# Two side products of a head pair change places: batch 1's queries into the third unit, the second half of its keys into the fourth unit's second step

## The chip, the cores and the metric

The kernel runs on one core of one Trainium2 chip. The metric is the device time of one execution in microseconds (us).

## What is computed

A gated layer: `x` (2 batches of 512 tokens, 512 wide, f32) is normed, attends to a context of 1024 tokens of 128 with 16 heads, and is added back under a gate; then a quantised feed-forward layer (512 to 2048 to 512) is added under a second gate. The change touches the attention alone:

```
q_hk = (hidden_q @ Wq.T).reshape(b, s, H, K)
q_big = jnp.einsum('bshk,hkq->bshq', q_hk, w_kc_q)
q_r = jnp.einsum('bshq,hqr->bhsr', q_big, W_qr)
k_r = jnp.einsum('bld,hdr->bhlr', kv_rope, W_kr)
scores = jnp.einsum('bhsr,bhlr->bhsl', q_r, k_r)
attn = jax.nn.softmax(scores, axis=-1)
ctx_c = jnp.einsum('bhsl,bld->bhsd', attn, kv_rope)
ctx_lat = jnp.einsum('bhsd,hkd->bshk', ctx_c, w_kc_kv)
out = ctx_lat.reshape(b, s, H * K) @ Wo.T
```

## The kernel before

The 16 heads are worked on as 8 pairs. Each pair goes through four units, w = 0 to 3: units 0 and 1 are batch 0, units 2 and 3 batch 1, each of 256 query rows for both heads (a buffer E of four 128x1024 tiles). The text calls them first to fourth unit. A unit has eight steps, c = 0 to 7, one per 128 tokens of context, and its steps are numbered from 0 as in the code, except where the change's own words say "second step" (c = 1).

In a step TensorE (`pe_pair`) does, in this order:

- the turn: four 128x128 transposes of E into one PSUM bank (L1350);
- at c = 3 and c = 7 a round of scores (L1297, twelve matmuls) for a unit ahead: at 3 the second half of the next unit, at 7 the first half of the one after it;
- the product of the turned probabilities and the context, two or three steps behind (L1308, L1309, L1310, three matmuls of 512 columns, into `ps_ctx`), none at c = 2, two rounds at c = 5;
- a side task, where the table `SIDE` names one: `("k", b, j)` is half j of the next pair's keys of batch b (L1249 to L1251, three matmuls), `("q", b)` the next pair's queries of batch b (L1270 to L1272, twelve matmuls), `("out", u, s)` the output rows of unit u (L1204 to L1206), `("m",)`, `("a",)` and `("b", h)` products of weights.

Every f32 operand is split into a high and a low part. So the turned bank is read twice: ScalarE copies it to `et_hi` (L1447) and VectorE writes the rest as `et_lo` (L1611), and only then is the bank free. The same goes for a side task of kind a, b, q or k: ScalarE's copy (`side_high`), then VectorE's subtraction (`side_low`, L1611 too). Both engines do this at the start of the step behind the task (`task_before`), ahead of that step's own turn. In between, ScalarE takes the exponential of a score tile at c = 0, 1, 4, 5 (L1490), VectorE a maximum over a score tile twice at c = 0, once at 3 and 4 (L1650), a reciprocal (L1655), and from pair 4 on the rounding of feed-forward weights at c = 5 and 7 (L1672); ScalarE takes those weights' sum or tanh (L1514) at some steps. GpSimd scales E (L1104) and, for pairs 5 and 6, reloads a split copy of x (`load_xn`, L1134).

Turns and side tasks share three PSUM banks in turn, in the order of the list that `bank_users` makes. A user waits until the one three places ahead of it has been read by VectorE:

```
def bank_before(variant, user):
    at = PLACE[variant][user] - BANKS
    ...
    return USERS[variant][at - PLACE0[variant]], False
```

Pairs are of three variants: the first (pair 0), the middle ones (1 to 6; pairs 1 to 3 are a loop of the hardware, 4 to 6 written out), and the last (pair 7), which has no next pair and leaves out m, a, q and k (`side_tasks`).

Of the kernel before, what the change touches and what calls it, by code (L numbers as in the profile page):

```python
# [81 lines left out]
SIDE = [  # L82
# [4 lines left out]
]  # L87
WK_AT = (1, 1)
KV1_AT = (1, 6)
# [1765 lines left out]
```

## Time and profile before

| | |
|---|---|
| runs | 738.93 us, median of 3 (737.99 to 739.98) |
| profiled execution | 739.03 us, its span 736.9 us |
| mean granted TensorE clock | 0.997 of 2.4 GHz |
| busy share of the span | TensorE matmul (PE) 98%, its weight loads (PEld) 72%, VectorE (DVE) 78%, ScalarE (ACT) 66%, GpSimd (POOL) 34% |

The span runs from the first to the last instruction. Busy times are sums over instructions; matmuls overlap in the pipeline (one of 512 columns is shown with 0.39 us while the next starts 0.23 us behind it), so a step's length is read from start to start. The windows view gives, for a stretch of the span, its length first, then each engine's busy time in it.

### The profile page before, as it was taken

What the parts mean: (1) busy time and instruction counts of PE and PEld (TensorE: products, weight loads), DVE (VectorE), ACT (ScalarE), POOL (GpSimd) and SP (SyncE); (2) the same over time, 40 slices, a digit from 0 to 9 for tenths busy, and PEclk for the clock granted to TensorE, in tenths of its full rate; (3) what the DMA queues carried; (4) which work ended last, traced back from release to release, by engine and by line L of the source; (5) the groups of instructions that cost most, each with busy time, mean ns of one, the idle gap of its engine ahead of it and who ended that gap; (6) DMA issues with size and microseconds to landing.
All of it is one profiled execution on the core that took longest, in us unless ns stands there. A gap on an engine that the chain in (4) does not pass through costs nothing.

```text
span 736.9 us, 11967 instructions
## 1 busy us (share of the span) xinstructions
PE 718.6 (98%) x4148; PEld 533.5 (72%) x4148; DVE 573.8 (78%) x1022; ACT 487.7 (66%) x821; POOL 252.8 (34%) x231
## 2 busy tenths in 40 slices
PE   8799999999999999999999999999999999999997
PEld 7577778777877787778778877787777776644553
DVE  5967777776778677776888787878787899999863
ACT  2578765666566656666666666666676756478876
POOL 5744422222222222222122222322322234677651
PEclk9999999999999999999999999999999999999999
DMA  8301073104011401040114212543250001000001
GB/s 303 121 2 58 29 271 143 59 29 157 28 57 28 157 28 57 28 157 31 58 57 146 70 59 103 181 155 120 67 195 4 29 1 57 1 1 29 16 29 44
DMA packets 22124, 58.31 MB, mean 79 GB/s; under 512 B 4033, under 2 KB 7233, under 8 KB 21313
## 3 DMA queue, kind: packets, MB, share of 16 engines
q1 hardware_dynamic: 20176, 45.49, 18.3%
q0 software_dynamic: 784, 10.49, 3.7%
q10 hardware_dynamic: 1120, 1.77, 0.7%
q8 instruction: 26, 0.43, 0.2%
q14 instruction: 18, 0.14, 0.1%
HBM read 51.45 MB, written 6.29 MB: 78 GB/s over the span
## 4 chain that ended last, share of the span: by engine, by line
PE 82%; DVE 9%; ACT 3%; POOL 2%; issue 2%; DMA 2%; POOLq 0%; DVEq 0%; ACTq 0%
PE ps_b L1350 14%; PE ps_s L1297 13%; PE ps_ctx L1308 9%; PE ps_ctx L1310 7%; PE ps_ctx L1309 7%; PE ps_s L568 4%; PE ps_b L1206 4%; PE ps_b L1204 4%; PE ps_b L1205 4%; PE ps_b L1270 2%; PE ps_b L619 2%; PE ps_b L1239 2%; PE ps_b L1272 2%; PE ps_b L1271 2%; PE ps_b L1276 2%
## 5 line engine op out<-in xcount | busy, mean ns | idle before, releaser
L1104 POOL TENSOR_SCALAR E<-E,small 128x1024 f32<-128x1024 f32 x128 | 149.1, 1165 | 418.1 <-DVE small L1655 418.1
L1447 ACT ACTIVATE et_hi<-ps_b 128x512 fp32r<-128x512 f32 x256 | 152.6, 602 | 164.3 <-PE ps_b L1350 164.2
L1611 DVE TENSOR_TENSOR et_lo<-ps_b,et_hi 128x512 fp32r<-128x512 f32 x256 | 175.5, 686 | 53.7 <-ACT et_hi L1447 52.0
L1650 DVE TENSOR_REDUCE small<-ps_s 128x1 f32<-128x1024 f32 x128 | 155.6, 1217 | 4.8 <-PE ps_s L1297 3.4
L1350 PEld LDWEIGHTS ps_b<-ident,E 128*128 128x128 f32 x1024 | 124.8, 140 | 40.0 <-issue 8.8
L1350 PE MATMUL ps_b<-ident,E 128*128 128x128 f32 x1024 | 152.3, 273 | 0.3 <-POOL E L1104 0.3
L1490 ACT ACTIVATE E<-ps_s,small 128x1024 f32<-128x1024 f32 x128 | 142.8, 1116 | 7.7 <-DVE small L1650 7.0
L1308 PE MATMUL ps_ctx<-et_hi,kv_hi 128*128 128x512 f32 x256 | 121.0, 473 | 0.5 <-DVE ctx_lo L1611 0.5
L1310 PE MATMUL ps_ctx<-et_lo,kv_hi 128*128 128x512 f32 x256 | 101.1, 395 | 0.0
L1309 PE MATMUL ps_ctx<-et_hi,kv_lo 128*128 128x512 f32 x256 | 100.5, 393 | 0.0
L1636 DVE SCALAR_TENSOR_TENSOR x_sb<-ps_b,small,x_sb 128x512 f32<-128x512 f32 x62 | 46.3, 746 | 28.5 <-PE ps_b L1206 28.5
L1308 PEld LDWEIGHTS ps_ctx<-et_hi,kv_hi 128*128 128x128 f32 x256 | 48.3, 189 | 24.8 <-issue 15.0
L568 PE MATMUL ps_s<-wq,q12T 128*128 128x512 fp8e4 x256 | 59.9, 379 | 1.3 <-issue 1.2
L1297 PE MATMUL ps_s<-k_hi,q_hi 64*128 64x512 f32 x256 | 57.5, 444 | 3.0 <-ACT E L1490 2.7
L1310 PEld LDWEIGHTS ps_ctx<-et_lo,kv_hi 128*128 128x128 f32 x256 | 48.0, 188 | 11.2
L1297 PE MATMUL ps_s<-k_hi,q_lo 64*128 64x512 f32 x256 | 51.0, 392 | 0.0
L1297 PE MATMUL ps_s<-k_lo,q_hi 64*128 64x512 f32 x256 | 51.0, 392 | 0.0
L1204 PE MATMUL ps_b<-b_hi,ctx_hi 128*128 128x512 f32 x128 | 50.4, 394 | 0.0
L1206 PE MATMUL ps_b<-b_lo,ctx_hi 128*128 128x512 f32 x128 | 50.3, 393 | 0.0
L1309 PEld LDWEIGHTS ps_ctx<-et_hi,kv_lo 128*128 128x128 f32 x256 | 48.8, 191 | 1.5
L1205 PE MATMUL ps_b<-b_hi,ctx_lo 128*128 128x512 f32 x128 | 49.9, 390 | 0.0
L510 POOL TENSOR_TENSOR hg<-h_f,E 128x512 f32<-128x512 f32 x32 | 40.5, 1272 | 22.5 <-DVE h_f L903 22.5
(187 smaller groups left out, 1078.4 us busy)
## 6 DMA issues: line engine op xcount, KB each, us to landing
w_stage<-in_wffn SPq DMA_DIRECT2D x48, 512.0 KB, 3.4
xnT<-xn_split POOLq DMA_DIRECT2D x3, 2048.0 KB, 9.6
wo_s<-in_woT SPq DMA_DIRECT2D x8, 512.0 KB, 7.1
xn_split<-xnT POOLq DMA_DIRECT2D x2, 2048.0 KB, 9.4
wq_s<-in_wq SPq DMA_DIRECT2D x7, 512.0 KB, 6.3
wkcq_s<-in_wkcqT SPq DMA_DIRECT2D x7, 384.0 KB, 4.1
x_sb<-in_x SPq DMA_DIRECT2D x4, 512.0 KB, 5.9
out<-x_sb SPq DMA_DIRECT2D x8, 256.0 KB, 2.0
```

What stands on the lines that cost most here:

```text
L568: last = nc.tensor.matmul(ps_s4[:, 2 * i + c % 2, :], q12T[:, k, i, d, :], wq8[:, DT * i + d, cols], start=(d == 0), stop=(d == DT - 1))
L1104: nc.gpsimd.tensor_scalar(e, e, rowinv[:, k:k + 1], 1.0, ALU.mult, ALU.mult).then_inc(scaled, 1)
L1204: nc.tensor.matmul(into, ctx_hi[:, u % 2, cols], b_hi[:, h, :], start=(h == 0), stop=False)
L1297: last = nc.tensor.matmul(ps_s[:, h, cols], q[head, b, rows], k[head, b, cols], start=(i == 0), stop=(i == 2))
L1308: nc.tensor.matmul(ps_ctx[:, :], kv_hi[:, b, c, :], et_hi[:, c % ET_RING, :], start=(c == 0), stop=False)
L1309: nc.tensor.matmul(ps_ctx[:, :], kv_lo[:, b, c, :], et_hi[:, c % ET_RING, :], start=False, stop=False)
L1310: nc.tensor.matmul(ps_ctx[:, :], kv_hi[:, b, c, :], et_lo[:, c % ET_RING, :], start=False, stop=(c == LT - 1))\
L1350: last = nc.tensor.transpose(into[:, s * P:(s + 1) * P], E[:, w % 2, s, c * P:(c + 1) * P], ident[:, :])
L1447: return nc.scalar.activation(out, in_, ACT.Copy)
L1490: nc.scalar.activation(E[:, w % 2, t, :], ps_s[:, t % 2, :], ACT.Exp, bias=negmax[:, k:k + 1], accum_out=rowsum[:, k:k + 1]).then_inc(exp_ ...
L1611: return nc.vector.tensor_tensor(out, full, hi.bitcast(F32), ALU.subtract)
L1650: nc.vector.tensor_reduce(negmax[:, k:k + 1], ps_s[:, t % 2, :], AX_X, ALU.max, negate=True).then_inc(max_done, 1)
```

## The change

Two entries of the table of side tasks move. `("q", 1)`, batch 1's queries of the next pair, goes from step 1 of the fourth unit to step 6 of the third. `("k", 1, 1)`, the second half of batch 1's keys, goes from step 3 of the fourth unit to step 1, the place that the queries leave.

```diff
 SIDE = [
     {0: ("m",), 2: ("a",), 4: ("out", 3, 0), 5: ("out", 3, 1), 6: ("b", 0)},
     {0: ("b", 1), 2: ("q", 0), 4: ("out", 0, 0), 5: ("out", 0, 1)},
-    {0: ("k", 0, 0), 1: ("k", 0, 1), 4: ("out", 1, 0), 5: ("out", 1, 1)},
-    {0: ("k", 1, 0), 1: ("q", 1), 3: ("k", 1, 1), 4: ("out", 2, 0), 5: ("out", 2, 1)},
+    {0: ("k", 0, 0), 1: ("k", 0, 1), 4: ("out", 1, 0), 5: ("out", 1, 1), 6: ("q", 1)},
+    {0: ("k", 1, 0), 1: ("k", 1, 1), 4: ("out", 2, 0), 5: ("out", 2, 1)},
 ]
```

The list of bank users, the counts that waits compare with and the places of ScalarE's and VectorE's copies all follow from this table. The number of instructions on each engine stays the same.

**TensorE, fourth unit of a pair, from the end of step 1 to the scores of step 3.** Before, the last of the queries' matmuls and the two turns:

```order
L1271 MATMUL ps_b<-xnT1,a_lo 128x512
L1272 MATMUL ps_b<-xnT1,a_hi 128x512
L1350 MATMUL ps_b<-ident,E 128x128 [waits side_freed]
L1350 MATMUL ps_b<-ident,E 128x128 x3
L1350 MATMUL ps_b<-ident,E 128x128 [waits et_split]
L1350 MATMUL ps_b<-ident,E 128x128 x3
L1297 MATMUL ps_s<-k_hi,q_hi 128x512 [waits exp_done]
```

Now:

```order
L1249 MATMUL ps_b<-kvT_hi,wk_hi 128x512 [waits wk_ready,et_split]
L1250 MATMUL ps_b<-kvT_hi,wk_lo 128x512
L1251 MATMUL ps_b<-kvT_lo,wk_hi 128x512
L1350 MATMUL ps_b<-ident,E 128x128 [waits side_freed]
L1350 MATMUL ps_b<-ident,E 128x128 x3
L1350 MATMUL ps_b<-ident,E 128x128 [waits et_split]
L1350 MATMUL ps_b<-ident,E 128x128 x3
L1297 MATMUL ps_s<-k_hi,q_hi 128x512 [waits exp_done]
```

The twelve query matmuls in front of the two turns have given way to three key matmuls. Both turns wait as before: that of step 2 for step 0's keys to be split (`side_freed`), that of step 3 for step 1's own turn (`et_split`).

**VectorE, fourth unit, from step 0's low part to that of step 3.** Before:

```order
L1611 TENSOR_TENSOR et_lo<-ps_b,et_hi 128x512 [waits ethi_done]
L1650 TENSOR_REDUCE small<-ps_s 128x1 [waits scores_done]
L1611 TENSOR_TENSOR k_lo<-ps_b,k_hi 128x512 [waits side_hi]
L1611 TENSOR_TENSOR et_lo<-ps_b,et_hi 128x512 [waits ethi_done]
L1655 RECIPROCAL small<-small 128x1 [waits exp_done]
L1611 TENSOR_TENSOR ctx_lo<-ps_ctx,ctx_hi 128x512 [waits ctxhi_done]
L1611 TENSOR_TENSOR q_lo<-ps_b,q_hi 128x512 [waits side_hi]
```

Now:

```order
L1611 TENSOR_TENSOR et_lo<-ps_b,et_hi 128x512 [waits ethi_done]
L1650 TENSOR_REDUCE small<-ps_s 128x1 [waits scores_done]
L1611 TENSOR_TENSOR k_lo<-ps_b,k_hi 128x512 [waits side_hi]
L1611 TENSOR_TENSOR et_lo<-ps_b,et_hi 128x512 [waits ethi_done]
L1655 RECIPROCAL small<-small 128x1 [waits exp_done]
L1611 TENSOR_TENSOR ctx_lo<-ps_ctx,ctx_hi 128x512 [waits ctxhi_done]
L1611 TENSOR_TENSOR k_lo<-ps_b,k_hi 128x512 [waits side_hi]
```

VectorE's work up to the context's low part is the same; behind it the keys' low part stands where the queries' stood. The row now reads as it does at the same place of the third unit, before and after.

## Rows read from the trace of the kernel before

**Rows 1.** The page: busy time, the span in 40 slices, the chain that ended last.

```profile
PE 718.6 (98%) x4148; PEld 533.5 (72%) x4148; DVE 573.8 (78%) x1022; ACT 487.7 (66%) x821; POOL 252.8 (34%) x231
...
PE   8799999999999999999999999999999999999997
...
PE 82%; DVE 9%; ACT 3%; POOL 2%; issue 2%; DMA 2%; POOLq 0%; DVEq 0%; ACTq 0%
```

**Rows 2.** Windows of pair 4: its third unit, then its fourth (length, busy per engine).

```profile
380.42:397.52 17.10, 17.10 (x100) 13.12 (x99) 14.47 (x25) 12.46 (x21) 4.75 (x4) 1.00 0.19 62
397.52:417.01 19.49, 19.49 (x111) 15.47 (x110) 15.22 (x26) 12.92 (x22) 4.75 (x4) 1.00 0.46 149
```

**Rows 3.** Windows: steps 0 to 3 of that third unit.

```profile
380.42:382.25 1.83, 1.83 (x11) 1.52 (x10) 1.73 (x3) 1.19 (x2) 0.00 (x0) 1.00 0.30 90
382.25:384.17 1.92, 1.92 (x12) 1.39 (x10) 1.92 (x4) 1.92 (x5) 0.00 (x0) 1.00 0.57 188
384.17:384.77 0.60, 0.60 (x6) 0.42 (x5) 0.60 (x2) 0.60 (x2) 0.00 (x0) 1.00 0.00 0
384.77:387.75 2.98, 2.98 (x21) 2.10 (x21) 1.97 (x5) 2.98 (x7) 1.29 (x2) 1.00 0.00 0
```

**Rows 4.** Windows: steps 0 to 3 of the fourth unit of pair 4.

```profile
397.52:399.34 1.82, 1.82 (x12) 1.52 (x11) 1.71 (x3) 1.19 (x2) 0.00 (x0) 1.00 0.47 137
399.34:403.21 3.87, 3.87 (x20) 3.21 (x19) 3.22 (x6) 3.13 (x7) 1.12 (x1) 1.00 0.94 290
403.21:403.64 0.43, 0.43 (x5) 0.43 (x4) 0.00 (x0) 0.23 (x1) 0.00 (x0) 1.00 0.96 334
403.64:407.27 3.63, 3.63 (x25) 2.61 (x23) 2.58 (x5) 2.38 (x4) 1.13 (x1) 1.00 0.68 235
```

**Rows 5.** Windows: a step without a side task (step 6, third unit, pair 4).

```profile
393.46:394.60 1.14, 1.14 (x9) 0.95 (x8) 0.75 (x1) 0.50 (x2) 0.92 (x1) 1.00 0.26 57
```

**Rows 6.** Timeline of steps 0 to 2, third unit, pair 4 (start, duration).

```profile
380.42 0.60 PE L1350 MATMUL ps_b<-ident,E 128*128 128x128 f32 x4
...
381.06 0.60 ACT L1447 ACTIVATE et_hi<-ps_b 128x512 fp32r<-128x512 f32 x1 [1.93 <-PE ps_b L1350]
...
381.69 0.69 DVE L1611 TENSOR_TENSOR et_lo<-ps_b,et_hi 128x512 fp32r<-128x512 f32 x1
...
382.30 1.22 DVE L1650 TENSOR_REDUCE small<-ps_s 128x1 f32<-128x1024 f32 x1
...
383.43 0.68 DVE L1611 TENSOR_TENSOR k_lo<-ps_b,k_hi 128x512 fp32r<-128x512 f32 x1
...
384.03 0.68 DVE L1611 TENSOR_TENSOR et_lo<-ps_b,et_hi 128x512 fp32r<-128x512 f32 x1
384.16 0.42 PEld L1350 LDWEIGHTS ps_b<-ident,E 128*128 128x128 f32 x4 [0.36 <-DVE k_lo L1611]
...
384.76 0.42 PEld L1350 LDWEIGHTS ps_b<-ident,E 128*128 128x128 f32 x4 [0.18 <-DVE et_lo L1611]
```

**Rows 7.** Who waited for whom: total us, times, longest us.

```profile
PEld ps_b L1350 <- DVE k_lo L1611: 2.5, 7, 0.4
...
PE ps_s L1297 <- ACT E L1490: 2.7, 2, 1.6
```

**Rows 8.** Timeline of VectorE around step 7 of the third unit, pair 4.

```profile
396.86 0.69 DVE L1672 TENSOR_SCALAR wq<-w_stage 128x1024 fp8e4<-128x1024 f32 x1
397.46 1.22 DVE L1650 TENSOR_REDUCE small<-ps_s 128x1 f32<-128x1024 f32 x1
398.78 0.69 DVE L1611 TENSOR_TENSOR et_lo<-ps_b,et_hi 128x512 fp32r<-128x512 f32 x1
```

**Rows 9.** Timeline of VectorE behind the queries, step 2, fourth unit, pair 4.

```profile
404.04 0.69 DVE L1611 TENSOR_TENSOR q_lo<-ps_b,q_hi 128x512 fp32r<-128x512 f32 x1 [0.84 <-ACT q_hi L1447]
404.65 0.68 DVE L1611 TENSOR_TENSOR et_lo<-ps_b,et_hi 128x512 fp32r<-128x512 f32 x1
```

**Rows 10.** Reload of x in pair 6: its issue, its landing, and step 6 there.

```profile
530.23 0.91 POOL L1134 DMA_DIRECT2D xnT<-xn_split  x1
...
DMA to landing us min/median/max: 9.5/9.6/10.8
...
544.03 0.27 PE L1350 MATMUL ps_b<-ident,E 128*128 128x128 f32 x1
```

## The prediction

> **What bounds the kernel now.** I read the page first. TensorE is busy for 98% of the span, its slices are full from end to end, and it holds 82% of the chain that ended last [rows 1]. Busy shares of a pipelined engine can flatter it, so I went on to the windows from the start of one step's turn to the start of the next, and compared steps with the same work. The middle pairs repeat to within 0.02 us per step, so pair 4 stands for the seven pairs, 0 to 6, that make queries and keys for a next pair.
>
> The step without a side task takes 1.14 us [rows 5]. Step 0 with its half of the keys takes 1.83 in the third unit and 1.82 in the fourth [rows 3, 4], so half the keys costs 1.82 - 1.14 = 0.68 to 0.70. Step 1 with the queries takes 3.87 [rows 4], so the queries cost 3.87 - 1.14 = 2.73. All of that is TensorE's own work, moved by the change and not removed. What can change is the waiting between.
>
> There are two kinds of place. In the fourth unit, where the twelve query matmuls stand in step 1, I find none: step 2 takes 0.43, a bare turn, and step 3 takes 3.63, which is a step of scores plus 0.70 for the keys [rows 4]. In the third unit, where two halves of the keys stand in steps 0 and 1, steps 1 to 3 take 1.92 + 0.60 + 2.98 = 5.50 [rows 3]. The same work priced from the fourth unit is 3.87 + 0.43 + 3.63 - 2.73 = 5.20 (it has one half of the keys among these steps too). So the third unit waits for 0.30 us in steps 1 to 3, and the fourth does not. The whole units agree roughly: 19.49 - 2.73 = 16.76 against 17.10 [rows 2], 0.34 with the ends of the windows in it.
>
> **Whose wait it is.** The timeline of the third unit shows a chain that begins with step 0's own turn [rows 6]. The turn starts at 380.42; ScalarE copies it from 381.06, VectorE writes its low part from 381.69, then takes the second maximum (382.30, 1.22 us long), then the keys' low part (383.43), then step 1's low part (384.03). Step 2's turn needs the bank of the keys and starts its weights at 384.16, as soon as that low part is out; step 3's turn needs the bank of step 1's turn and starts its weights at 384.76, as soon as that is out. The wait for the keys' low part is listed 7 times, 2.5 us together [rows 7]: once in each of the seven pairs, so it is no accident of pair 4. The 0.36 us that the weight load stood idle [rows 6] is longer than what the matmuls lost, since loads run ahead. I take the loss from the windows.
>
> **The change part by part.**
>
> Keys into step 1 of the fourth unit. This removes the 2.73 us of query matmuls that lay over exactly this chain. Afterwards the fourth unit's steps 0 to 3 hold turn, keys, turn, keys, turn, turn, scores, as the third unit's do, with the same work for ScalarE and VectorE in the same order. The chain is tied to step 0's turn, so what comes ahead of it hardly matters. Step 2's turn now waits for the keys of step 0, step 3's for the turn of step 1. Cost: 0.30 us per pair, from [rows 3, 4]. Bounds: no less than 0, if something shortens the chain; no more than the 0.36 + 0.18 = 0.54 us that the two weight loads stood idle [rows 6]. I take 0.30, since it is the same pattern in the same pair.
>
> The Trainium skill, page Perfetto Trace Analysis, section Optimizing Tensor Performance, says that independent groups of matmuls should rotate through different PSUM banks, so that reading one out overlaps the next group's matmuls. The kernel still rotates through its three banks after the change, so by that rule the sum would be 0. The third unit rotates in the same way and waits all the same, which speaks against it here.
>
> Keys out of step 3 of the fourth unit. The 0.70 us moves with them. Nothing that follows in steps 4 to 7 leaned on it: the third unit has no side task in its step 3 either. Gain 0, cost 0.
>
> Queries into step 6 of the third unit. 2.73 us of TensorE's work goes there. Their bank was last used by step 5's turn, three places back, and its low part is long out. Steps 6 and 7 there show no wait that the queries could cover: step 6 is the 1.14 us step itself [rows 5]. So gain 0. Behind them, ScalarE and VectorE have to read the queries out ahead of step 7's turn. After the queries of pair 4, step 2's turn started at 403.21 [rows 4], the queries' low part at 404.04 and the turn's at 404.65, ending at 405.33, 2.12 us behind [rows 9]. In the third unit the chain must be through the rounding (0.69) and the first maximum (1.22) by the time that the low part of the next unit's step 0 starts. Before, the rounding starts at 396.86 and the maximum ends at 398.68, 0.10 us ahead of the low part at 398.78 [rows 8], with step 7's turn at 394.60 [rows 5]. With the queries the rounding would start at about 394.60 + 2.12 = 396.72, a little sooner than the 396.86 of before (VectorE's operations overlap by under 0.1 us). Cost 0; if I am wrong and the whole 0.69 us of the extra low part comes on top, 0.69 - 0.10 = 0.59 us in each of the three pairs with rounding, 1.8 us.
>
> The reload of x. In pair 6 it is issued at 530.23 and lands up to 10.8 us later, at 541.0; the queries now read it from 544.03 + 1.14 = 545.2 [rows 5, 10], some 6 us sooner than from step 1 of the fourth unit, and 4 us behind the landing. SP's and POOL's own waits on the queries are met sooner, and no DMA is issued in another order. Cost 0.
>
> Sum: 7 x 0.30 = 2.1 us. The profiled execution (739.03 us, its span 736.9 and 2.1 around it) becomes 741.1; it lay 0.10 above the median of the runs, so against that I say 738.93 + 2.1 = **741.0 us**, slower by 0.28%.
>
> **The rivals.**
>
> *No difference.* The queries' 2.7 us ahead of step 7 let ScalarE and VectorE catch up before the fourth unit, and the chain comes out short enough that no turn waits. For it: VectorE is busy for only 78%. Against it: in the third unit step 0's low part starts at 381.69, right behind ScalarE's copy of the turn (381.06 + 0.60) [rows 6], so VectorE was not behind there either, and the chain still came out long, because it starts with the turn itself. Time 738.9. This is also what the rule on rotating banks, in the Trainium skill's Perfetto Trace Analysis, would give.
>
> *Faster.* Scores wait for exponentials of the unit ahead, and the queries now stand ahead of the scores of step 7. The waits list such a wait for 2.7 us in all, in 2 places [rows 7]. If both were covered: 738.9 - 2.7 = 736.2. It decides only if those two lie in front of step 7 of a third unit; in pair 4 no such wait shows. The Trainium skill, Perfetto Trace Analysis, Identifying the Most-Contended Engine, says that a matmul's busy share is no good measure and that of the weight loads is better. By the 72% for those, TensorE has room, and covering others' work in front of the scores could pay. The steps' equal lengths from pair to pair say that it has none in these stretches.
>
> *Slower than that.* The queries' reading out comes on top in front of the first maximum, and the chain of the fourth unit starts 0.59 us late in three pairs: 2.1 + 1.8 = 3.9, 742.8. It decides if VectorE's low part of step 7 ends more than 0.1 us later, counted from step 7's turn, than the 396.86 of before.
>
> *The reload is late.* It stalls the queries in pairs 5 and 6 from 4 us of delay on; nothing in the traffic moves, so I give it next to nothing.
>
> **How the numbers follow.** The forecast mechanism gets 0.76, no difference 0.10, faster 0.04, slower than that (late reload included) 0.10. A measurement of this kernel tells about 0.3%, 2.2 us, from no change, and the forecast lies just below it, at 2.1. Of its 0.76 I put 0.42 within and 0.34 above. So: faster 0.05, same 0.52, slower 0.43. The range goes from 739.5, where only step 1's 1.92 - 1.83 = 0.09 us comes seven times [rows 3], to 742.8, the sum with the extra low part; it leaves out the faster rival and most of no difference.
>
> **What would show it.** In the profile after, the windows of the fourth unit's steps 1 to 3 should read 1.92, 0.60 and 2.98, as the third unit's do now, and the wait of the turn for the keys' low part should stand 14 times in place of 7, with about 5 us. Step 6 of the third unit should take 3.87 and step 7 no more than the 2.92 us from 394.60 to 397.52 [rows 4, 5]. A pair should grow by 0.30. Wrong would be: fourth-unit steps 1 and 2 at 1.82 and 0.43 (no difference); a longer step 7, or a step 1 above 1.92 (the slower rival); a pair shorter than before (the faster one).

## The result and the profile after

The changed kernel takes 740.69 us (median of 20 runs, 738.6 to 742.28), the kernel before 738.17 (median of 20, 736.58 to 740.33). The ratio is 1.0023, with an interval of 1.0013 to 1.0032. Timed a second time, beside the experiments, it was 1.0035 (1.0022 to 1.0047), 740.82 us beside 738.35, where I had expected 1.0029. The change makes the kernel slower: by 1.7 and 2.6 us going by the two ratios, by 2.5 going by the medians each time, and by 2.2 in the traces, as shown below. The forecast was 2.1.

The page of the changed kernel; its lines answer to [rows 1]:

```profile
PE 721.4 (98%) x4148; PEld 533.4 (72%) x4148; DVE 573.8 (78%) x1022; ACT 488.1 (66%) x821; POOL 253.1 (34%) x231
...
PE 83%; DVE 8%; ACT 3%; issue 2%; POOL 2%; DMA 2%; POOLq 0%; DVEq 0%; ACTq 0%
```

The busy share tells nothing: TensorE is shown as 98% busy in both, and even the 0.60 us of a step 2 that waits count as busy in full. The lengths of the windows tell it. First pair 4's third and fourth unit whole, then steps 0 to 3 of the fourth, then steps 6 and 7 of the third (columns as in [rows 2]):

```profile
381.89:401.72 19.83, 19.83 (x112) 15.41 (x110) 15.28 (x26) 13.09 (x22) 4.77 (x4) 1.00 0.15 54
401.72:418.80 17.08, 17.08 (x99) 13.13 (x98) 14.20 (x24) 12.41 (x21) 4.75 (x4) 1.00 0.51 170
401.72:403.55 1.83, 1.83 (x11) 1.52 (x10) 1.49 (x2) 1.20 (x2) 0.00 (x0) 1.00 0.55 195
403.55:405.46 1.91, 1.91 (x11) 1.38 (x10) 1.91 (x4) 1.91 (x5) 0.00 (x0) 1.00 0.94 340
405.46:406.06 0.60, 0.60 (x6) 0.42 (x5) 0.60 (x2) 0.60 (x3) 0.00 (x0) 1.00 1.17 208
406.06:409.04 2.98, 2.98 (x21) 2.09 (x20) 1.97 (x5) 2.98 (x6) 1.36 (x2) 1.00 1.02 335
394.93:398.80 3.87, 3.87 (x21) 3.21 (x20) 1.51 (x3) 1.64 (x2) 2.03 (x2) 1.00 0.36 135
398.80:401.72 2.92, 2.92 (x21) 2.06 (x19) 2.10 (x4) 1.09 (x2) 0.00 (x0) 1.00 0.00 0
```

Steps 1, 2 and 3 of the fourth unit are now those of the third [rows 3], 1.91, 0.60 and 2.98 us, 5.49 together. The third unit's step 6 has grown from 1.14 by the queries' 2.73 to 3.87, and step 7 is 2.92 as before. The two units together went from 17.10 + 19.49 = 36.59 [rows 2] to 19.83 + 17.08 = 36.91, 0.32 more.

The waits view names the same wait twice as often as in [rows 7]:

```profile
PEld ps_b L1350 <- DVE k_lo L1611: 5.0, 14, 0.4
...
PE ps_s L1297 <- ACT E L1490: 2.7, 2, 1.6
```

The pair as a whole, the window from the first turn of pair 4 to the first of pair 5, of the kernel before and of the changed one:

```profile
341.51:417.01 75.50, 75.48 (x439) 59.03 (x438) 60.97 (x101) 50.47 (x86) 19.00 (x16) 1.00 0.24 78
```

```profile
342.95:418.80 75.85, 75.84 (x439) 58.96 (x438) 60.76 (x101) 50.59 (x86) 19.05 (x16) 1.00 0.23 78
```

The pair begins 1.4 us later in the second. Most of that is the change's own doing in pairs 0 to 3, 1.28 us together; 0.16 us is there already at pair 0's first turn and has nothing to do with it. To keep such differences at the start out, the table below gives the time from pair 0's first turn to pair 7's last turn, read from each trace: 593.9 us before, 596.2 after, 2.2 more (593.92 and 596.15 before rounding). What follows the last turn is 100.7 us in both.

### The profile page after: what moved, and what is told of

The parts are those of the page before. It is cut to its first block, busy times and chain, and to the rows that moved or that the text cites. A ratio compares the mean times of both kernels' runs of the same rounds, so it can differ in the third digit from the quotient of the medians.

```text
span 739.3 us, 11967 instructions
## 1 busy us (share of the span) xinstructions
PE 721.4 (98%) x4148; PEld 533.4 (72%) x4148; DVE 573.8 (78%) x1022; ACT 488.1 (66%) x821; POOL 253.1 (34%) x231
## 4 chain that ended last, share of the span: by engine, by line
PE 83%; DVE 8%; ACT 3%; issue 2%; POOL 2%; DMA 2%; POOLq 0%; DVEq 0%; ACTq 0%
PE ps_b L1350 14%; PE ps_s L1297 13%; PE ps_ctx L1308 9%; PE ps_ctx L1310 7%; PE ps_ctx L1309 7%; PE ps_s L568 4%; PE ps_b L1206 4%; PE ps_b L1204 4%; PE ps_b L1205 4%; PE ps_b L1270 2%; PE ps_b L619 2%; PE ps_b L1239 2%; PE ps_b L1272 2%; PE ps_b L1271 2%; PE ps_b L1276 2%
## 5 line engine op out<-in xcount | busy, mean ns | idle before, releaser
L1350 PE MATMUL ps_b<-ident,E 128*128 128x128 f32 x1024 | 153.9, 274 | 0.3 <-POOL E L1104 0.3
```

What stands on the lines that cost most here:

```text
L1350: last = nc.tensor.transpose(into[:, s * P:(s + 1) * P], E[:, w % 2, s, c * P:(c + 1) * P], ident[:, :])
```

## The experiments

Each is a build of its own; the diffs are against the kernel before unless said otherwise. "Pairs" is the time from the first to the last turn.

| kernel | ratio to before (interval) | pairs, us | pair 5, us |
|---|---|---|---|
| before | | 593.9 | 75.3 |
| the change | 1.0023 (1.0013 to 1.0032), again 1.0035 (1.0022 to 1.0047) | 596.2, again 596.1 | 75.6 |
| keys ahead, queries stay | one run: 740.42 beside 740.03 | 594.1 | 75.3 |
| queries alone | one run: 741.34 | 597.7 | 75.8 |
| queries in step 7 | one run: 750.15 | 606.0 | 77.0 |
| batch 0's queries in step 1 | 0.9987 (0.9976 to 0.9997) | 594.3 | 75.6 |
| and a in step 1 | 0.9957 (0.9944 to 0.9971), again 0.9965 (0.9948 to 0.9982) | 591.0, again 590.9 | 75.0 |
| and m in step 1 | 0.9953 (0.9937 to 0.9969), again 0.9933 (0.9913 to 0.9953) | 589.7 | 74.7 |

### Which of the two moves costs: keys ahead, queries stay

```diff
-    {0: ("k", 0, 0), 1: ("k", 0, 1), 4: ("out", 1, 0), 5: ("out", 1, 1)},
-    {0: ("k", 1, 0), 1: ("q", 1), 3: ("k", 1, 1), 4: ("out", 2, 0), 5: ("out", 2, 1)},
+    {0: ("k", 0, 0), 1: ("k", 0, 1), 4: ("out", 1, 0), 5: ("out", 1, 1), 6: ("k", 1, 1)},
+    {0: ("k", 1, 0), 1: ("q", 1), 4: ("out", 2, 0), 5: ("out", 2, 1)},
```

> From the kernel before, the other exchange: batch 1's queries stay in step 1 of the fourth unit, and the second half of batch 1's keys goes from its step 3 into step 6 of the third unit. My theory (a wait appears only where steps 0 to 2 of a unit are too short to cover the chain turn, copy, low part, maximum, keys' low part): no wait is added, fourth unit's steps 1 to 3 are 3.87, 0.43 and 2.93 us, step 6 of the third unit is 1.14 + 0.70 = 1.84, a pair 75.3 us as before, the time within 1 us of the kernel before. Rival (any side task ahead of step 7 delays what VectorE owes the fourth unit): step 1 or 2 of the fourth unit longer by 0.1 to 0.6 us, 1 to 4 us in all.

The windows of pair 4, step 6 of the third unit and steps 1 to 3 of the fourth:

```profile
394.94:396.77 1.83, 1.83 (x11) 1.52 (x10) 1.31 (x2) 1.19 (x2) 0.93 (x1) 1.00 0.49 145
401.51:405.38 3.87, 3.87 (x20) 3.21 (x19) 3.22 (x6) 3.06 (x7) 1.13 (x1) 1.00 0.95 300
405.38:405.82 0.44, 0.44 (x6) 0.43 (x5) 0.00 (x0) 0.24 (x1) 0.00 (x0) 1.00 1.09 350
405.82:408.75 2.93, 2.93 (x22) 2.03 (x21) 1.89 (x4) 2.37 (x4) 0.98 (x1) 1.00 0.78 273
```

All as my theory had it. A side task in step 6 of the third unit costs its own work and no more, and taking the second half of the keys out of step 3 neither gains nor loses. With the queries left in step 1 there is no wait.

### The queries alone

The table's third row gets `6: ("q", 1)` as in the change, the fourth becomes:

```diff
+    {0: ("k", 1, 0), 3: ("k", 1, 1), 4: ("out", 2, 0), 5: ("out", 2, 1)},
```

> Only the queries move (to step 6 of the third unit); the second half of the keys stays in step 3 of the fourth, whose step 1 is then bare. My theory: the wait comes from taking the queries away, not from bringing the keys. Step 3's turn would now arrive 1.83 + 1.14 + 0.43 = 3.40 us behind step 0's turn and must wait for the keys' low part, out at 3.74, and the scores behind it for the exponential that ends at about 4.5: 0.35 to 0.6 us per pair, 2.5 to 4.2 us in all, so 1.0031 to 1.006 of the kernel before. Rival (the two halves of the keys behind one another are what holds up ScalarE and VectorE): no wait, the time of the kernel before.

Steps 1 to 3 of the fourth unit of pair 4:

```profile
402.81:403.94 1.13, 1.13 (x9) 0.96 (x8) 1.13 (x2) 1.13 (x4) 0.00 (x0) 1.00 0.98 325
403.94:404.72 0.78, 0.60 (x6) 0.36 (x4) 0.78 (x3) 0.78 (x2) 0.00 (x0) 1.00 0.94 366
404.72:408.50 3.78, 3.73 (x22) 2.65 (x23) 2.56 (x6) 3.15 (x6) 2.17 (x2) 1.00 1.03 322
```

Step 2 is 0.35 longer than a bare turn, step 3 0.15 longer than in [rows 4] (3.63). A pair takes 75.83, 0.52 above the 75.31 of before, inside the 0.35 to 0.6 that was expected. The one timed run does not show as much: 741.34 beside 740.03 is 1.3 us more, under the 2.5 that I had as the least, while the pairs in the traces take 3.8 us more. So taking the queries out of step 1 is what costs; the keys put there by the change give 0.2 us of it back as cover.

### The same place for less: the queries in step 7

As the change, with `7: ("q", 1)` in place of `6: ("q", 1)`.

> As the change, but the queries stand in step 7 of the third unit, behind its scores and right ahead of the fourth unit. If VectorE only needs time to catch up ahead of the fourth unit, this place gives it as much and the first maximum can be done ahead of the turn: the fourth unit's steps 1 to 3 no longer than 5.5 us. My theory (fixed order on VectorE and ScalarE: the queries' low part stands ahead of the first maximum and of step 0's low part): the chain starts some 1.3 us later, the exponentials too, and scores at step 3 wait for the second: about 2 us more per pair than the fourth unit has without waits, some 14 us in all, 752 to 753.

VectorE from the end of the third unit on, pair 4 (the fourth unit's turn starts at 406.19):

```profile
407.02 0.69 DVE L1611 TENSOR_TENSOR q_lo<-ps_b,q_hi 128x512 fp32r<-128x512 f32 x1 [3.54 <-ACT q_hi L1447]
407.63 1.22 DVE L1650 TENSOR_REDUCE small<-ps_s 128x1 f32<-128x1024 f32 x1
408.76 0.68 DVE L1611 TENSOR_TENSOR et_lo<-ps_b,et_hi 128x512 fp32r<-128x512 f32 x1
409.36 1.22 DVE L1650 TENSOR_REDUCE small<-ps_s 128x1 f32<-128x1024 f32 x1
410.61 0.69 DVE L1611 TENSOR_TENSOR k_lo<-ps_b,k_hi 128x512 fp32r<-128x512 f32 x1
```

VectorE stood idle for 3.54 us while the queries ran, with the scores of the first maximum ready, because the queries' low part comes ahead of it in its order. Step 0's low part then starts 2.57 us behind its turn, in place of 1.27 [rows 6], and step 1 of the fourth unit takes 3.33. The direction and the mechanism were right, the size too high: a pair takes 77.02, 1.7 us more than before and not 2, and all pairs 12.1 and not 14; the scores came no later than the turns that stood ahead of them, so the extra wait on the exponential that I had added did not come.

### Which link of the chain: a late maximum, late exponentials, both

All three are against the changed kernel, edits of two small tables:

```diff
-MAX_STEP = {0: 1, 3: 2, 4: 3}
+MAX_STEP = {1: 1, 3: 2, 4: 3}
```

```diff
-EXP_STEP = {0: 0, 1: 1, 4: 2, 5: 3}
-INV_STEP = {1: 0, 2: 1, 5: 2, 6: 3}
+EXP_STEP = {1: 0, 2: 1, 4: 2, 5: 3}
+INV_STEP = {2: 0, 3: 1, 5: 2, 6: 3}
```

> The change, with the second maximum of every unit taken in step 1, behind that step's low part, in place of step 0. My theory (that maximum, 1.22 us, is the link that makes the keys' low part late): the waits of steps 2 and 3 for low parts vanish in third and fourth units (0.43 for step 2 in place of 0.60), but the second exponential comes some 1.8 to 2 us later and the scores of step 3, which wait for it, stall for 1.5 to 1.9 us in each third and fourth unit: about 3 us more per pair than the change, some 22 us in all. Rival (the keys' low part is late because of ScalarE's copy or the matmuls, not that maximum): step 2 stays at 0.60.

> The change, with the first two exponentials of every unit one step later (steps 1 and 2 in place of 0 and 1), the maxima as they were. If VectorE's second maximum is a link of its own, step 2 of the third and fourth units stays at about 0.60, the keys' low part coming behind that maximum as before. If only ScalarE's exponential was (its copy of the keys stands behind it), step 2 falls to 0.43 to 0.50. The scores of step 3 stall for the later exponential by 2 to 3 us in either case, some 30 to 40 us in all.

> The change, with both the second maximum (to step 1) and the first two exponentials (to steps 1 and 2) later. If the two links run side by side and either alone makes the turns wait, as the version with the late maximum alone suggests (step 2 still 0.54 there), then only here do both go: step 1 1.83, step 2 0.43 to 0.48 in the third and fourth units. If the wait has a third cause (the copies themselves, the banks' order), step 2 stays above 0.50. Step 3 stalls for the exponentials by 2.5 to 3 us, some 38 us in all.

Steps 1 and 2 of the third unit of pair 3, first with the late maximum, then with the late exponentials, then with both:

```profile
321.98:323.82 1.84, 1.84 (x12) 1.45 (x11) 0.95 (x3) 1.48 (x4) 0.00 (x0) 1.00 0.00 0
323.82:324.35 0.53, 0.53 (x6) 0.36 (x5) 0.53 (x3) 0.00 (x0) 0.00 (x0) 1.00 0.00 0
```

```profile
325.29:327.21 1.92, 1.92 (x12) 1.39 (x10) 1.92 (x4) 1.72 (x3) 0.00 (x0) 1.00 0.00 0
327.21:327.81 0.60, 0.60 (x6) 0.42 (x5) 0.54 (x1) 0.60 (x3) 0.00 (x0) 1.00 0.00 0
```

```profile
321.86:323.70 1.84, 1.84 (x12) 1.52 (x10) 1.14 (x3) 1.64 (x3) 0.00 (x0) 1.00 0.00 0
323.70:324.13 0.43, 0.43 (x5) 0.43 (x4) 0.43 (x2) 0.43 (x3) 0.00 (x0) 1.00 0.00 0
```

The maximum alone brings step 1 from 1.91 to 1.84 and step 2 to 0.53 (in the third units of pairs 4 to 6 it stays at 0.60), the exponentials alone bring nothing, and only both bring step 2 to a bare turn. So there are two links side by side: VectorE's second maximum, ahead of the low parts of the keys and of step 1's turn, and ScalarE's first exponential, ahead of the copies of the same two. My expectation for the late maximum (0.43 for step 2) was wrong; it had one link only.

None of the three is a way to a faster kernel. The scores of step 3 wait for the second exponential, and the runs (one of each kernel) took 780.68, 783.96 and 780.07 us beside 740.03, 738.35 and 738.35 of before. I had expected some 22 us over the change for the first, and it was 40. The stall itself is as expected, 1.9 us (step 3 takes 4.82 in pair 3). What I had left out are pair 7, whose short steps stall more (7.2 us), the first unit of each middle pair (0.55 us), and what the clock did (last section). The other two lie 43 and 39 us over the change, where I had 30 to 40 and 38, but for partly wrong reasons: their step 3 stalls for 1.9 and 2.2 us, less than the 2 to 3 and the 2.5 to 3 expected.

### The other way: long work into step 1 everywhere

If the queries' 2.73 us in step 1 hide the wait, batch 0's queries should do the same in the third unit. They need the keys' place, and the keys go to the second unit's step 6:

```diff
-    {0: ("b", 1), 2: ("q", 0), 4: ("out", 0, 0), 5: ("out", 0, 1)},
-    {0: ("k", 0, 0), 1: ("k", 0, 1), 4: ("out", 1, 0), 5: ("out", 1, 1)},
+    {0: ("b", 1), 4: ("out", 0, 0), 5: ("out", 0, 1), 6: ("k", 0, 1)},
+    {0: ("k", 0, 0), 1: ("q", 0), 4: ("out", 1, 0), 5: ("out", 1, 1)},
```

> From the kernel before: batch 0's queries go from step 2 of the second unit to step 1 of the third, where the second half of batch 0's keys stood; that half goes to step 6 of the second unit. If long work in step 1 is what covers the chain, the third unit loses its 0.30 us of waits as the fourth has none. The second unit's step 2 is then bare: the 0.30 us that the queries waited there go, and the turns of steps 2 and 3 wait as in pair 7's second unit (0.62 and 3.10, 0.37 in all). Net 0.23 us per pair less, 1.6 us in all: ratio 0.998. Rival (VectorE has a fixed debt per unit that shows somewhere): no gain, ratio 1.000 to 1.003.

The ratio is 0.9987 (0.9976 to 0.9997), a smaller gain than expected, and in the trace the pairs take no less time but 0.4 us more (594.3). The trace fits the rival's "no gain", the timed runs do not reach it; this difference stays open. Of pair 5, steps 2 and 3 of the second unit, then steps 1 to 3 of the third:

```profile
438.85:439.47 0.62, 0.60 (x6) 0.36 (x4) 0.62 (x2) 0.62 (x2) 0.00 (x0) 1.00 0.00 0
439.47:443.06 3.59, 3.08 (x19) 2.09 (x20) 3.27 (x7) 3.36 (x7) 1.17 (x2) 1.00 0.01 2
455.36:459.25 3.89, 3.89 (x20) 3.20 (x19) 3.22 (x6) 3.06 (x7) 0.00 (x0) 1.00 0.23 82
459.25:459.69 0.44, 0.44 (x6) 0.44 (x5) 0.00 (x0) 0.24 (x1) 0.00 (x0) 1.00 0.00 0
459.69:462.62 2.93, 2.93 (x22) 2.04 (x21) 1.89 (x4) 2.37 (x4) 2.70 (x3) 1.00 0.58 129
```

The third unit lost its wait, as expected. The second unit has a new one, larger than the 3.10 that I took from pair 7: step 3 takes 3.54 to 3.61 in five of the seven pairs. In that window the waits view gives 0.5 us to the first product of step 3, for the context's low part. Pair 7 has no weights to split in its second unit, and the others have (`WK_AT`), which was missing in my sum. But the split alone is not it: pairs 2 and 6 do it too, and their step 3 takes 3.09 and 3.10. The weights' low part on VectorE is what differs, here in pair 5 and then in pair 6:

```profile
440.28 1.13 POOL L1104 TENSOR_SCALAR E<-E,small 128x1024 f32<-128x1024 f32 x1 [6.13 <-DVE small L1655]
440.36 1.19 DVE L1611 TENSOR_TENSOR wk_lo<-wkr_s,wk_hi 128x128 fp32r<-128x128 f32 x1 [0.28 <-ACT wk_hi L1447]
```

```profile
515.86 1.28 POOL L1104 TENSOR_SCALAR E<-E,small 128x1024 f32<-128x1024 f32 x1 [6.13 <-DVE small L1655]
515.93 0.29 DVE L1611 TENSOR_TENSOR wk_lo<-wkr_s,wk_hi 128x128 fp32r<-128x128 f32 x1 [0.28 <-ACT wk_hi L1447]
```

The same subtraction takes 0.29 us in the two short pairs and 1.04 to 1.19 in the five long ones. In the long ones it ends just behind GpSimd's scaling of E (0.13 to 0.14 us in each), which started ahead of it; in the short ones the scaling is the one that takes longer, 1.28 us. So the two engines get in each other's way, and with starts 0.07 us apart (0.22 in pair 0) it is now the one and now the other that is held up. Pairs 2 and 6 take 75.07, 0.24 less than before, which is the 0.23 of my sum; the other five lose some 0.5 us each to this. With long work in the second unit's step 1, in the next version, it costs nothing: step 1 takes 2.92 whether the subtraction takes 0.29 (pair 5) or 1.18 (pair 6).

Long work into the second unit's step 1 as well, the product a:

```diff
-    {0: ("m",), 2: ("a",), 4: ("out", 3, 0), 5: ("out", 3, 1), 6: ("b", 0)},
-    {0: ("b", 1), 4: ("out", 0, 0), 5: ("out", 0, 1), 6: ("k", 0, 1)},
+    {0: ("m",), 4: ("out", 3, 0), 5: ("out", 3, 1), 6: ("b", 0)},
+    {0: ("b", 1), 1: ("a",), 4: ("out", 0, 0), 5: ("out", 0, 1), 6: ("k", 0, 1)},
```

> The version before this one, and the product ('a',) goes from step 2 of the first unit to step 1 of the second, between its product ('b', 1) and step 2. My theory: 1.8 us of TensorE's work in step 1 covers the second unit's chain as well, so all of 0.30 + 0.31 us of waits per pair go, and step 2 of the first unit, bare now, arrives at 2.48 + 1.14 = 3.62 and step 3's turn at 4.05, behind the keys' equivalent 3.75: no new wait. 0.6 us per pair, 4.2 us in all: 734.7 where before has 738.9, ratio 0.9943. Rival: the first unit's bare step 2 lets its scores arrive ahead of the second exponential, and 0.1 to 0.5 us per pair come back: ratio 0.995 to 0.999.

Of pair 5, steps 2 and 3 of the first unit, then steps 1 to 3 of the second:

```profile
415.86:416.29 0.43, 0.43 (x5) 0.43 (x4) 0.31 (x1) 0.43 (x2) 0.00 (x0) 1.00 0.00 0
416.29:419.49 3.20, 2.99 (x22) 2.03 (x20) 1.81 (x5) 3.20 (x6) 1.48 (x2) 1.00 0.00 0
432.12:435.04 2.92, 2.92 (x25) 2.78 (x24) 2.65 (x5) 2.92 (x8) 0.36 (x1) 1.00 0.12 48
435.04:435.47 0.43, 0.43 (x6) 0.43 (x5) 0.23 (x2) 0.40 (x2) 0.43 (x1) 1.00 0.00 0
435.47:438.40 2.93, 2.93 (x21) 2.06 (x20) 2.27 (x5) 2.38 (x4) 1.47 (x2) 1.00 0.01 3
```

The second unit is free of waits, 0.43 and 2.93. The rival's 0.28 us came in the first unit: step 3 takes 3.20 in place of 2.92, its scores waiting for the second exponential. A pair takes 74.99, and the kernel is faster than before, 0.9957: the rival's range, not the 0.9943 of my theory.

The last 0.28 us, with m in step 1 of the first unit. In this order m, not a turn, takes the bank that the mean's product used ahead of pair 4, so it has to wait for its reader:

```diff
-    {0: ("m",), 4: ("out", 3, 0), 5: ("out", 3, 1), 6: ("b", 0)},
+    {1: ("m",), 4: ("out", 3, 0), 5: ("out", 3, 1), 6: ("b", 0)},
...
                         wait_bank(pe, p, variant, tasks[c])
+                        if mean and PLACE[variant][tasks[c]] == BANKS - 1:
+                            pe.wait_ge(mean_chain, 1)
```

> The version with ('a',) in step 1 of the second unit left 0.28 us of wait in step 3 of the first unit (3.20 in place of 2.92), scores waiting for the second exponential. Here ('m',) goes from step 0 to step 1 of the first unit, and its matmuls take the wait for the mean's bank that a turn had. My theory: step 1's turn, copy, maximum and exponential all come 1.3 us sooner against the scores, whose arrival stays, so the 0.28 us go: a pair 74.7 us, 0.6 us per pair less than the kernel before in seven pairs, 4.2 us: ratio 0.9940 (0.9930 to 0.9950). Rival (the exponential is late for VectorE's sake, whose two maxima stand in step 0 in any case): step 3 stays at 3.2, ratio 0.9957.

Steps 0 to 3 of the first unit of pair 5:

```profile
414.79:415.91 1.12, 1.12 (x8) 0.95 (x7) 1.12 (x2) 0.49 (x1) 0.00 (x0) 1.00 0.08 26
415.91:418.39 2.48, 2.48 (x21) 2.35 (x20) 2.37 (x5) 2.24 (x5) 0.00 (x0) 1.00 0.59 200
418.39:418.82 0.43, 0.43 (x6) 0.43 (x5) 0.15 (x2) 0.43 (x1) 0.08 (x1) 1.00 0.00 0
418.82:421.74 2.92, 2.92 (x22) 2.07 (x20) 1.71 (x6) 2.79 (x6) 1.33 (x2) 1.00 0.00 0
```

Step 3 is back at 2.92 and a pair takes 74.71 (in pair 4, where step 2 of the first unit takes 0.99 in place of 0.44, the pair takes 75.34). The measured ratio, 0.9953, did not tell this version from the one above, so both were run again together:

> The version with ('a',) in step 1 of the second unit, once more, now on the same chip as the next one. Its first trace has 591.0 us from the first turn of pair 0 to the last turn of pair 7, the kernel before 593.9: 2.9 us less, ratio 0.996 again.

> The version with ('m',) in step 1 as well. Its first trace has 589.7 us from the first turn of pair 0 to the last of pair 7, 1.3 us less than the version above. If the parts ahead of and behind the pairs do not depend on it, it should be 0.9978 to 0.9990 of the version above here, ratio 0.9943 to the kernel before. Rival (what the pairs gain is lost ahead of them, where its first trace had pair 0 start 3 us later): no difference between the two.

They came out at 0.9965 (0.9948 to 0.9982), 735.23 us, and 0.9933 (0.9913 to 0.9953), 734.22 us. The traces say 591.0 and 590.9 us for the pairs without m in step 1, and 589.7 twice with it. The two intervals overlap a little in the second timing and lie over one another in the first, so the 1.2 to 1.3 us between the two versions are shown for the pairs by the traces and not settled for the whole by the timed runs. My rival is not settled either: in both profiled executions with m in step 1, pair 0 starts 3.3 to 3.5 us later than in the two without, and their whole spans are 2 us longer (733.6 and 733.8 against 731.6 and 731.5). Against the kernel before, both are faster beyond their intervals, each time.

## Why the prediction was right

**The bound.** Comparing steps of equal work, from turn to turn, held throughout: units that hide everything cost the same in every kernel (1.13 for the plain step, 2.73 for the queries, 0.70 for a half of the keys), and the differences followed above sit in single steps. That the middle pairs repeat to within 0.02 us per step has two exceptions, neither in a step that the sum uses: step 2 of pair 4's first unit (2.43 in place of 2.22) and step 7 of pair 3's fourth (3.05 in place of 2.92), before and after alike.

**Keys into step 1, queries out of it: 0.30 us per pair.** Measured 5.49 against 5.20 in pair 4, and 2.23 us over all pairs, 0.32 per pair, against 2.1. The step was right, and not by luck in the sum: the seven pairs give 0.29 to 0.37 each, and pair 7 gives 0.02; that taking the queries away is what costs, and that the pattern of the third unit prices it, the two exchanges (queries stay, queries alone) show apart from each other.

**Keys out of step 3, and a side task in step 6: nothing.** Right on both, 2.93 and 1.83 us in the first experiment.

**Queries ahead of step 7.** Right. In the changed kernel VectorE around step 7 of the third unit of pair 4 (its turn at 398.80) reads:

```profile
399.62 0.69 DVE L1611 TENSOR_TENSOR q_lo<-ps_b,q_hi 128x512 fp32r<-128x512 f32 x1 [2.67 <-ACT q_hi L1447]
400.23 0.68 DVE L1611 TENSOR_TENSOR et_lo<-ps_b,et_hi 128x512 fp32r<-128x512 f32 x1
400.83 0.68 DVE L1672 TENSOR_SCALAR wq<-w_stage 128x1024 fp8e4<-128x1024 f32 x1
401.43 1.22 DVE L1650 TENSOR_REDUCE small<-ps_s 128x1 f32<-128x1024 f32 x1
402.98 0.69 DVE L1611 TENSOR_TENSOR et_lo<-ps_b,et_hi 128x512 fp32r<-128x512 f32 x1 [0.34 <-ACT et_hi L1447]
```

The rounding starts 2.03 us behind the turn, where I had worked out 2.12 and before it was 2.26. The first maximum ends 0.33 us ahead of the low part, in place of 0.10: where the slower rival would have struck there is more room than before.

**The reload of x.** No wait on it shows in either trace.

**The chain.** Half right. The prediction followed VectorE alone, from the turn's copy over the maximum to the keys' low part. The runs with the late maximum and the late exponentials show ScalarE's exponential as a second link of nearly the same length. The price did not hang on it, since it was taken from the pattern and not from the links, but an edit aimed at the maximum alone would have been mispriced, and one of my expectations was.

**The rivals.** No difference fell with the doubled wait, 14 times in place of 7. Faster fell with the scores' wait, 2.7 us in 2 places before and after: both lie in pair 7, which makes no queries, so the queries did not stand in front of them. Scores that lose time to an exponential do exist, but in another unit and another order (the 0.28 us of the first unit, above).

**The rule on rotating banks** (the Trainium skill, Perfetto Trace Analysis, Optimizing Tensor Performance) would, read as the prediction read it, have given no loss, and the runs decide against that here: rotating three banks hides a reading out by two engines in a row only if enough matmuls lie in between, here some 3.7 us from step 0's turn to the release of its keys' bank (384.16 - 380.42 in [rows 6]), and the order of the side tasks is what puts them there.

## What to carry to other kernels

In a schedule written by hand, long work that depends on nothing belongs where the other engines' chain is longest, not where it looks free: the same twelve matmuls cost nothing extra in either place, and their cover is worth 0.3 us per unit only in one. When a task moves away, look for another place in the same program that already has the order that it leaves behind, and price the loss from there. An engine that is 98% busy may still be worth 0.5% by order alone, and the windows from step to step show it where busy shares do not.

## What the runs showed of the hardware beyond that

**A stall of about 2 us can cost more than itself.** In the kernels with late exponentials some steps took 1.5 us more than their equals in other pairs. Steps 3 and 4 of the fourth unit of pair 1, in the kernel with both late:

```profile
184.77:190.76 5.99, 3.85 (x21) 2.46 (x20) 4.84 (x8) 3.17 (x8) 2.23 (x2) 0.83 0.01 3
190.76:193.96 3.20, 3.20 (x15) 2.70 (x13) 1.48 (x2) 1.69 (x3) 0.00 (x0) 0.78 0.00 0
```

TensorE had stood idle for 2.14 us ahead of these scores. The granted clock of the windows is 0.83 and 0.78, so part of each ran at 1.2 and not 2.4 GHz: from 188.77 to 192.04 matmuls of 512 columns show up to 0.63 us in place of 0.39 (0.79 in place of 0.48 for the first of a product), and then they recover. TensorE had taken up work again at 187.50, 1.3 us ahead of the fall. It happened in the fourth unit of five of the seven pairs and not in the other two, with about the same stall. The kernel before never shows it within the pairs. Why the same stall is followed by a fall of the clock in some units and not in others is not shown.

**The runs' scatter lies ahead of the pairs.** Pair 0's first turn comes at 42.3 us before, 42.5 and 41.4 in two traces of the change, 39.8 and 39.9 with a in step 1 and 43.1 and 43.4 with m in step 1; the list of tasks ahead of it (`PROLOGUE_TASKS`) is the same in all of them. The granted clock separates the traces: in five of all 14 it never falls to 1.2 GHz ahead of that turn, which then comes at 39.7 to 40.9 us; in the other nine it does, once or twice for 3.4 us, and the turn comes at 41.3 to 43.7. From 30 to 40 us the kernel before has a granted clock of 0.83 and the 39.8 us trace 1.00:

```profile
30.00:40.00 10.00, 8.90 (x36) 5.77 (x37) 6.58 (x10) 4.92 (x9) 5.76 (x5) 0.83 0.30 105
```

```profile
30.00:40.00 10.00, 9.82 (x52) 6.10 (x53) 7.65 (x12) 5.77 (x11) 4.99 (x4) 1.00 0.33 105
```

Whether the fall of the clock or another delay comes first there is not shown. A difference of 2 us between two kernels is of the size of what differs in this stretch from execution to execution, while the pairs' time repeats to 0.2 us in the three kernels that were profiled twice. Here the profile is the finer instrument. The timed runs bear it out for the change and for the two faster versions; for batch 0's queries in step 1, where they say 0.13% less and the pairs' time 0.4 us more, they do not.
